# Second pass of a linear-attention plus gated-linear-attention block: low-rank parts split from PSUM, den and q/z moved back, dense state products per head

## The reference

```
x = x + layernorm(attention(layernorm(x)))
x = x + layernorm(ffn(layernorm(x)))

attention: q, k, v = split(x @ w_qkv.T); q, k = relu(q), relu(k)      16 heads of 32
           z = 1 / (sum_n k . q + eps);  out = ((v k^T) q) * z;  out @ w_proj.T + b_proj
ffn:       8 heads of 64, chunks of 64 rows
           q1, k1, v = x@Wq, x@Wk, x@Wv;  q2 = x@Wqa@Wqb;  k2 = softmax(x@Wka@Wkb)
           gk1, gk2 = log_sigmoid(x@Wg.a@Wg.b + bg.)/16
           e = softmax(x@We) (4 experts, the largest alone is kept)
           o = chunk_gla(q1, k1, v, gk1) + sum_e chunk_gla(q2*fac_e, k2*fac_e, v, gk2*mask_e)
           o = rmsnorm(o) * norm_w * silu(x@Wga@Wgb);  o @ Wo
```

## Time and profile before

| | |
|---|---|
| median of 3 runs | 3093.59 us (3091.72 to 3103.98) |
| the profiled execution | 3092.17 us, of which the span in the trace is 3090.3 us |
| busy in the span | TensorE 2785.3 us (90%), its weight loads 1743.0, VectorE 2041.1 (66%), ScalarE 1646.9 (53%), GpSimd 1358.3 (44%) |
| mean granted TensorE clock | 0.979 of full speed |
| chain of waits that ended last | TensorE 71%, VectorE 19%, ScalarE 7% |

### The profile page before, as it was taken

How to read it: one execution, slowest core, us unless ns; L and a number is a source line. 1 busy time by engine, 2 the same in 40 slices (tenths; PEclk the granted TensorE clock), 3 DMA queues, 4 the chain that set the end, 5 groups by cost and what they waited for, 6 DMA issues and landing times.

```text
span 3090.3 us, 56322 instructions
## 1 busy us (share of the span) xinstructions
PE 2785.3 (90%) x20720; PEld 1743.0 (56%) x20720; DVE 2041.1 (66%) x3878; ACT 1646.9 (53%) x3281; POOL 1358.3 (44%) x1006
## 2 busy tenths in 40 slices
PE   6999899998999999999879998989999999999997
PEld 3444466655666655666534445555666655665555
DVE  4442677777777777677544426777777777677775
ACT  4332565555565565555433325555655565556653
POOL 2873344444444444444422334444444444444444
PEclk9999899999999999999989999999999999999999
DMA  4221000000000000000021210000000000000000
GB/s 174 62 95 41 18 21 20 20 20 20 20 20 20 20 20 20 20 20 20 18 86 58 68 41 18 21 20 20 20 20 20 20 20 20 20 20 20 20 20 11
DMA packets 48376, 97.49 MB, mean 32 GB/s; under 512 B 5376, under 2 KB 5376, under 8 KB 47680
## 3 DMA queue, kind: packets, MB, share of 16 engines
q1 hardware_dynamic: 37008, 68.44, 6.8%
q10 hardware_dynamic: 9792, 17.83, 1.6%
q0 software_dynamic: 1520, 10.50, 0.9%
HBM read 63.19 MB, written 33.55 MB: 31 GB/s over the span
## 4 chain that ended last, share of the span: by engine, by line
PE 71%; DVE 19%; ACT 7%; issue 2%; POOL 1%; DMA 0%; POOLq 0%; ACTq 0%; DVEq 0%; SPq 0%
PE psum L448 10%; PE psum L303 10%; PE psum L305 9%; PE psum L304 9%; PE psum L546 5%; DVE region L1115 5%; PE psum L423 4%; PE psum L437 4%; PE psum L457 4%; PE psum L413 4%; DVE region L1212 2%; DVE region L1172 2%; ACT ogT L729 2%; PE psum L312 2%; PE psum L430 2%
## 5 line engine op out<-in xcount | busy, mean ns | idle before, releaser
L976 POOL TENSOR_TENSOR region<-region,kfac 128x512 f32<-128x512 f32 x64 | 66.7, 1043 | 821.4 <-DVE kfac L1191 821.4
L958 POOL TENSOR_TENSOR region<-region,mb 128x512 f32<-128x512 f32 x256 | 322.6, 1287 | 73.4 <-ACT region L619 72.9
L991 POOL TENSOR_TENSOR region<-region,decay 64x1280 f32<-64x1280 f32 x128 | 298.1, 2329 | 117.5 <-DVE decay L1207 112.2
L448 PE MATMUL psum<-region 128*128 128x128 f32 x2560 | 317.3, 286 | 10.8 <-POOL region L958 10.8
L448 PEld LDWEIGHTS psum<-region 128*128 128x128 f32 x2560 | 309.1, 202 | 11.1 <-issue 11.1
L303 PE MATMUL psum<-wb,region 128*128 128x512 f16 x768 | 292.5, 381 | 1.1 <-DVE mb L1156 1.1
L304 PE MATMUL psum<-wb,region 128*128 128x512 f16 x768 | 292.0, 380 | 0.0
L305 PE MATMUL psum<-wb,region 128*128 128x512 f16 x768 | 291.9, 380 | 0.0
L971 POOL TENSOR_SCALAR region<-region,m 128x512 f32<-128x512 f32 x256 | 172.3, 692 | 267.7 <-DVE hm L1140 192.0
L950 POOL TENSOR_TENSOR region<-region 128x1024 f32<-128x1024 f32 x64 | 146.6, 2291 | 288.2 <-DVE region L1306 230.7
L1306 DVE SCALAR_TENSOR_TENSOR region<-psum,region 128x512 f16<-128x512 f32 x64 | 44.2, 691 | 261.7 <-ACT region L790 261.7
(11 more groups left out here) (233 smaller groups left out, 7595.1 us busy)
## 6 DMA issues: line engine op xcount, KB each, us to landing
region<-x_in SPq DMA_DIRECT2D x128, 256.0 KB, 2.7
q_cols<-region ACTq DMA_DIRECT2D x64, 256.0 KB, 2.3
region<-q_cols SPq DMA_DIRECT2D x64, 256.0 KB, 2.9
out_rows<-region SPq DMA_DIRECT2D x60, 256.0 KB, 2.0
region<-wb_in POOLq DMA_DIRECT2D x1, 3072.0 KB, 12.1
region<-wqkv_in SPq DMA_DIRECT2D x4, 512.0 KB, 5.3
region<-wqkv_in POOLq DMA_DIRECT2D x2, 1024.0 KB, 5.6
region<-wproj_in POOLq DMA_DIRECT2D x2, 1024.0 KB, 7.4
```

Of the source, the lines that this page charges most:

```text
L448: last = mm(bank[7][:, pr * P:(pr + 1) * P], q, state[:, pr, path, :], start=(pr == 0 and path == 0), stop=False, skip_group_check=True)
L958: last = nc.gpsimd.tensor_tensor(qm[:, e, :, :], q2T, mb[:, e, :].unsqueeze(1).to_broadcast([P, PAIRS, P]), ALU.mult)
L991: nc.gpsimd.tensor_tensor(state[h, :, :, h], carry[h, :, :, :], decay[h, :, :].unsqueeze(3).to_broadcast([D2, PAIRS, PATHS, D2]), ALU.mult ...
```

## The change

- ScalarE's `front_low` copies the logits first, and then writes the high parts of `low` straight from bank 7 in three instructions. VectorE's `front_low` computes the low parts with bank 7 as one input; the buffer `lowf` is gone (and the region is 256 words smaller).
- On VectorE the first half of `front_router` (largest logit, differences, score) now runs ahead of `front_low`; its second half is the new function `front_label`, behind `front_low`.
- On TensorE `project_q` is split; the order is now k, q2, den, q1.
- On ScalarE `ahead_z` moves from ahead of `back_square` to behind `front_sig`. On VectorE `ahead_qz` moves from ahead of `back_norm` to just ahead of `ahead_qz_split`.
- The dense state products are 8 matmuls of 64 columns by 64 columns, one for each head, into the lower or upper 64 partitions of bank 1, in place of 4 of 128 by 128 of which half was used; `back_carry1` reads them from there.

```diff
             def state_products(n, p, ahead):
                 for pr in range(PAIRS):
-                    mm(bank[1][:, pr * P:(pr + 1) * P], k1g[:, pr * P:(pr + 1) * P], v[:, p, pr * P:(pr + 1) * P], start=True, stop=True)
+                    for odd in range(2):
+                        h = 2 * pr + odd
+                        mm(psum[odd * D2:odd * D2 + D2, 1, pr * D2:(pr + 1) * D2],
+                           k1g[:, h * D2:(h + 1) * D2], v[:, p, h * D2:(h + 1) * D2], start=True, stop=True)
 # TensorE step
                 if back:
                     inter(m)
                     intra(m, mp)
+                if front:
+                    project_k(n)
+                    project_q2(n)
                 if ahead:
                     den(n + 1, mp)
                 if front:
-                    project_k(n)
-                    project_q(n)
+                    project_q1(n)
 # ScalarE
             def front_low(n):
                 act.wait_ge(S("low_pe"), cur(n))
-                act.wait_ge(S("low_ok"), prev(n))
-                ac(lowf[:, 0, :], bank[7][:, 0:P], ACT.Identity, bias=one_rows, scale=1.0 / (W_SCALE * S_SCALE))
-                ac(lowf[:, 1, :], bank[7][:, P:2 * P], ACT.Copy, scale=1.0 / (W_SCALE * S_SCALE)).then_inc(S("low1_ok"), 1)
+                act.wait_ge(S("q1_pe"), prev(n))
                 ac(logit_s, bank[7][:, 2 * P:2 * P + NEXP], ACT.Copy, scale=1.0 / W_SCALE).then_inc(S("low0_ok"), 1)
+                ac(low[up, 0:4:2, :], parts[up], ACT.Copy, scale=LOW_SCALE)
+                ac(low[down, 1, :], parts[down, 0, :], ACT.Identity, bias=one_rows[down, :], scale=LOW_SCALE)
+                ac(low[down, 3, :], parts[down, 1, :], ACT.Copy, scale=LOW_SCALE).then_inc(S("low1_ok"), 1)
 # VectorE
             def front_low(n):
                 dve.wait_ge(S("low1_ok"), cur(n))
-                dve.wait_ge(S("q1_pe"), prev(n))
-                ve.tensor_copy(low[up, 0:4:2, :], lowf[up, :, :])
-                ve.tensor_copy(low[down, 1:4:2, :], lowf[down, :, :])
-                ve.tensor_copy(low[g_copy, 1, :], lowf[g, 0, :]).then_inc(S("lowh_ok"), 1)
-                dve.wait_ge(S("lowh_ok"), n + 1)
-                ve.tensor_tensor(low[g_low, 1, :], lowf[g, 0, :], low[g, 1, :], ALU.subtract)
-                ve.tensor_tensor(low[down, 0:4:2, :], lowf[up, :, :], low[up, 0:4:2, :], ALU.subtract)
-                ve.tensor_tensor(low[up, 3, :], lowf[down, 1, :], low[down, 3, :], ALU.subtract).then_inc(S("low_ok"), 1)
+                ve.scalar_tensor_tensor(low[down, 0:4:2, :], parts[up], LOW_SCALE, low[up, 0:4:2, :], *minus)
+                ve.scalar_tensor_tensor(low[g_low, 1, :], parts[g, 0, :], LOW_SCALE, low[g, 1, :], *minus)
+                ve.tensor_scalar(low[g_copy, 1, :], parts[g, 0, :], LOW_SCALE, None, ALU.mult)
+                ve.scalar_tensor_tensor(low[up, 3, :], parts[down, 1, :], LOW_SCALE, low[down, 3, :], *minus).then_inc(S("low_ok"), 1)
 # VectorE step
                 if front:
+                    front_router(n)
                     front_low(n)
-                    front_router(n)
+                    front_label(n)
...
-                if ahead:
-                    ahead_qz(n + 1, mp)
                 if back:
                     back_norm(m)
...
                 if ahead:
+                    ahead_qz(n + 1, mp)
                     ahead_qz_split(n + 1)
```

More of the change, by code:

```diff
@@ L36 @@
 NEXP = 4
-REGION = 13316
+REGION = 13060
 PATHS = 1 + NEXP
@@ L49 @@
 S_SCALE = 8.0
+LOW_SCALE = 1.0 / (W_SCALE * S_SCALE)
 REGION2 = 13056
@@ L139, in sandwich_kernel @@
         xnT, qz16 = cut(2, KT, P, dt=f16), cut(2, KT, P, dt=f16)
-        logit_s, lowf = cut(4), cut(2, P)
+        logit_s = cut(4)
         low = cut(4, P, dt=f16)
@@ L380, in project_k, with project_q2, project_q1 @@
                     mm3(bank[0], lambda x: xnT[:, x, g, :], lambda x: wb[:, x, g, C:2 * C], g == 0, g == KT - 1)
-            def project_q(n):
+            def project_q2(n):
                 pe.wait_ge(S("ls_ok"), cur(n))
                 second(bank[4], 2, 3)
+            def project_q1(n):
                 wide(n, 5, 0, "q1_pe")
@@ L651, in front_low @@
                 act.wait_ge(S("low_pe"), cur(n))
-                act.wait_ge(S("low_ok"), prev(n))
-                ac(lowf[:, 0, :], bank[7][:, 0:P], ACT.Identity, bias=one_rows, scale=1.0 / (W_SCALE * S_SCALE))
-                ac(lowf[:, 1, :], bank[7][:, P:2 * P], ACT.Copy, scale=1.0 / (W_SCALE * S_SCALE)).then_inc(S("low1_ok"), 1)
+                act.wait_ge(S("q1_pe"), prev(n))
+                up, down = slice(0, LORA), slice(LORA, P)
+                parts = bank[7][:, 0:2 * P].rearrange("p (x c) -> p x c", x=2)
                 ac(logit_s, bank[7][:, 2 * P:2 * P + NEXP], ACT.Copy, scale=1.0 / W_SCALE).then_inc(S("low0_ok"), 1)
+                ac(low[up, 0:4:2, :], parts[up], ACT.Copy, scale=LOW_SCALE)
+                ac(low[down, 1, :], parts[down, 0, :], ACT.Identity, bias=one_rows[down, :], scale=LOW_SCALE)
+                ac(low[down, 3, :], parts[down, 1, :], ACT.Copy, scale=LOW_SCALE).then_inc(S("low1_ok"), 1)
             def front_router(n):
@@ L743, in step @@
                     front_ke(n)
-                if ahead:
-                    ahead_z(n + 1)
                 if back:
@@ L753, in step @@
                     front_sig(n)
+                if ahead:
+                    ahead_z(n + 1)
                 if back:
@@ L1097, in back_carry1 @@
                     h = slice(odd * D2, odd * D2 + D2)
-                    last = ve.tensor_tensor(carry[h, :, 0, :], bank[1][h, :].rearrange("p (a b) -> p a b", a=PAIRS)[:, :, h],
+                    last = ve.tensor_tensor(carry[h, :, 0, :], bank[1][h, 0:PAIRS * D2].rearrange("p (a b) -> p a b", a=PAIRS),
                                             state[h, :, 0, h], ALU.add)
@@ L1130, in front_router, with front_label @@
                 ve.scalar_tensor_tensor(lscore[:, :], ldiff[:, :], 0.0, score, ALU.is_equal, ALU.mult).then_inc(S("lscore_ok"), 1)
+            def front_label(n):
                 dve.wait_ge(S("lscore_ok"), n + 1)
```

2 lines of the change are left out of this document (added).

## The result

After the change the kernel takes **3114.03 us** (median of 7 runs, 3112.43 to 3115.69), beside 3092.08 us before on the same chip (7 runs, 3091.72 to 3103.98). The ratio is 1.0057, with a 95% interval of 1.0042 to 1.0071: **slower by half a percent, 22 us**. The prediction was 3057 us, with 7% on slower. The kernel before ran in 3071 to 3104 us over all comparisons. So each experiment has its ratio to before from its own comparison, and where kernels of different comparisons are set beside one another, their times stand beside the ratios.

A forecast was written before the change was run, and what follows sets the result against it. TensorE, busy 90%, was taken to bound the kernel, with two VectorE-made gaps. From 3092.2: second gap -65.4, gates 0, dense 0, clock falls +31, giving 3057 us; range 2945 to 3105.

The forecast's parts named there:

- What bounds the kernel, the two gaps and their makers: TensorE, 90% busy, waits each step 2.21 us before the gates and 1.11 us before the result's transposes, for VectorE's splits.
- I expect L1130 to miss its turn: On VectorE the router's score misses its start by a 0.03 us margin and waits for GpSimd's 2.43 us sum.
- Splits 1.33 us behind it, gap unchanged: VectorE's four splits end 1.33 us after the score, as late as before, so TensorE's gates gap stays: 0.0 us gained.
- The second gap, -65.4 us: TensorE's wait ahead of the result's transposes goes: 1.09 us a step over 60 steps, 65.4 us.
- The gates term of 0: The wait ahead of the gates on TensorE gains 0.0 us a step, bounds -2.21 and +0.4.
- Cover for z, q/z and its split: The later z, q/z and split stay hidden, done about 1052.0 with y_mm needing them about 1054.3: 2.3 us of cover.
- Dense at 0.8 us: TensorE's dense state products take 0.8 us for 0.98, bounds -0.5 and +0.75, worth nothing as the gates gap follows.
- I take 17 of 62: TensorE's clock falls to half behind the gates' wait in 17 of 62 steps: 52 us, +31 against before.
- rival 2: Clock falls behind the gates' wait, widened by quicker dense products, eat the gain: 3128 us at 40 steps; 7%.

The follow-up runs named there:

- e8: The kernel before with only the low-rank split from PSUM, router, q/z and dense products as they were: 2939.3 us, ratio to before 0.9507.
- e5: The kernel after with GpSimd's sum of the masked scores cut to 8 of 1024 columns, VectorE's order kept: 2872.41 us, ratio to before 0.9289.
- e1: The kernel after with the router's score moved behind the four splits, maximum and difference still ahead: 2859.99 us, ratio to before 0.9297.
- e10: The kernel before with eight unread products ahead of v filling the gates' gap, nothing else: 3076.4 us, ratio to before 0.9963.
- e7: The kernel before with the q/z part and eight unread products ahead of v filling the gates' gap: 3013.46 us, ratio to before 0.9748.
- e6: The kernel after with the old dense state products and the whole router behind the splits: 2873.38 us, ratio to before 0.9294.
- e9: The kernel after with the whole router (maximum, difference and score) behind the splits: 2860.94 us, ratio to before 0.9272.
- e3: The kernel before with the q/z part of the change alone: 3126.34 us, ratio to before 1.0164.
- e4: The kernel after with the dense state products as they were before: 3079.7 us, ratio to before 1.0001.
- e12: The kernel after with eight unread products in project_k, away from the gates' gap, lengthening the step to 37.57 us: 3104.34 us, ratio to before 1.0054.
- e2: The kernel after with eight unread products ahead of v filling the gates' gap: 3007.42 us, ratio to before 0.9777.
- e11: The kernel before with two unread products ahead of k's, the step staying at 37.5 us: 3097.09 us, ratio to before 1.0014.

## Why the prediction was wrong

- **What bounds the kernel, the two gaps and their makers**: right. e8 and e5 show the first one to be VectorE held by GpSimd, and e1 shows both gone at 2860 us.
- **"I expect L1130 to miss its turn"**: right, by 0.13 us in the step shown (1082.23 against 1082.10); the median of 64 is 2260 ns, the least, in the first step, 164. The difference met the instruction ahead of the sum and was late, as reasoned.
- **Splits 1.33 us behind it, gap unchanged**: 1084.53 to 1085.84 is 1.31; 2.38 us of gap for a forecast of about 2.35.
- **The second gap, -65.4 us**: right; 62.9 us between e10 and e7. The gates term of 0 was off by little: the steps of after are another 0.13 us shorter than those of e7 (36.31 for 36.44), -8 us, and the stretches outside the 60 steps took 8 us more. Cover for z, q/z and its split was enough: y_mm got no wait.
- **Dense at 0.8 us**: 0.60, nearer to the lower end of 0.47 than I took it. Worth nothing behind a gap, as said, and 12 us once the gap is gone (e6 and e9), where the transposes ahead of the products give back 0.09 us a step.
- **The clock, "I take 17 of 62"**: this step failed, the term for the clock behind the gates' wait. 52 falls, 108 us for a forecast of 52 us: +87 in place of +31, which is 56 of the 57 us of error. That the rest comes to 1 us is luck, -8 and +8 as above. It is rival 2 that came true, at 3114 for the 3128 worked out with 40 steps: more falls, but 30 of them at 1.55 us and 20 at 3.1, where I had priced each at 3.07. Its reason, a gap widened by quicker dense products, was not the cause: e3 has the gap of before and 56 falls, e4 the old dense products and 46.

How the step went wrong: I had 8 falls in 62 steps of one kernel and scaled them by gap length, "about twice as many for a wait that is at least as long". The count does not follow the gap there: 8 and 56 at 2.2 us (before, e3), 8 and 52 at 2.38 (e12, after). The base was weak too: 8 is the count of one execution. Its four falls in the second pass came after 20 equal steps, with six more behind them, not at the end of it as I had written, and the longest of the three runs on hand, 3103.98 us, already stood 12 us above the one I counted in. The sentence ahead of it, "with another step length and a gap a little longer that comes again differently; ends are 0 and every step", was the right one. With both ends open the term is 0 to about 190 us (62 at 3.07), and a likeliest value near the low end had no row behind it. A gain of 65 us that leaves such a term free was worth far less than 76% on faster, and the range had to reach past 3105.

What is shown and what isn't: that the falls follow the gates' gap (e2, e7, e10: filled, none is left behind it), that its holder is GpSimd's sum (e5), that the q/z part brings them (e3), and that a longer step at the same gap and the same busy share changes their number (e12). Why 36.3 and 36.4 us draw 46 to 56 falls, 37.5 draws 4 to 8 and 38.0 draws 15 is not; the regular cycles speak for an alignment that hangs on the length of the step, and that stays open.

## What to carry to other kernels

An idle gap of TensorE that recurs every step has two prices, its length and what the clock does behind it; if the clock falls behind even a few of them, treat the number of falls after any change of step length as unknown, from none to all, and close or fill the gap before judging anything else. Ahead of a critical chain on VectorE, put no instruction with two inputs in SBUF, and no copy or tensor_scalar on SBUF, however small, while GpSimd works: its price is what is left of GpSimd's running instruction. The maximum, a reduction with one input in SBUF, paid nothing. And test parts separately: here the split alone was -5%, the q/z part alone +1.6%, all with the router moved +0.6%, and without that move -7.3%. A kernel whose count of falls varies, like before, moves by 1% from one execution to the next (3071 to 3104 us); count the falls in the trace beside it.

## What the runs showed of the hardware

- An instruction of 4 columns waited 2.26 us for GpSimd (164 ns alone); scalar_tensor_tensor with one input in PSUM kept its 0.42 us beside the same GpSimd instruction (e1), and a reduction of 4 columns in SBUF its 157 ns in all steps, 62 of them beside GpSimd (after).
- With a gap of 2.1 to 2.4 us per step, half-clock stretches stood behind 8 of 62 gaps at a step of 37.54 us (4 in e11's trace) and of 37.57 us, 15 at 37.97, 56 at 36.44, 52 at 36.31 and 46 at 36.32 (e4, gap 2.08). With 0.5 to 0.6 us of gap in its place there were none (e2, e7, e10), and none with a gap of 1.1 us elsewhere in the step (e8).
- A fall added about 1.55 or 3.1 us to a step, and nearly nothing between: the lengths of steps come in three classes, and in after in a cycle of six steps.
- 16 instructions with 64-column weights and 64 columns, in two halves of the array in turn, take 0.60 us, 37 ns each; 8 with 128 by 128 took 0.98. The float32 transposes ahead of them took 1.84 us in place of 1.75.
